# A mixture of experts with the layer norms at its two ends and its routing in one pass over the chunks, and roots as a power on GpSimd

## What is computed

```python
def _layernorm(x, axis=-1, eps=1e-05):
    m = jnp.mean(x, axis=axis, keepdims=True)
    v = jnp.var(x, axis=axis, keepdims=True)
    return (x - m) / jnp.sqrt(v + eps)

# stage 6, E = 8 experts, the two best kept
probs = jax.nn.softmax(jnp.einsum('bsh,eh->bse', x, router_w), axis=-1)
weights, indices = jax.lax.top_k(probs, K)
weights = weights / (weights.sum(axis=-1, keepdims=True) + 1e-06)
gate, up = jnp.split(jnp.einsum('bsh,ehi->bsei', x, w13), 2, axis=-1)
y = jnp.einsum('bsei,eih->bseh', jax.nn.silu(gate) * up, w2)

# stage 7 begins with
x = resid * lax.rsqrt(jnp.mean(resid * resid, -1, keepdims=True) + EPS) * norm_w

# stage 8, experts kept while the sorted probabilities sum to under 0.8
h = jax.nn.relu(jnp.einsum('bth,ehf->betf', x, W1) + b1[None, :, None, :])
y = jnp.einsum('betf,efh->beth', h, W2) + b2[None, :, None, :]
return jnp.einsum('bte,beth->bth', gate, y)
```

## Time and profile before

| | us |
|---|---|
| median of three runs | 2854.76 |
| lowest, highest | 2851.32, 2855.35 |
| the profiled execution | 2854.67 |
| its span, first to last instruction | 2852.9 |

### The profile page before, as it was taken

The page is one execution under the profiler, slowest core; times in us unless marked ns, Lnnn a source line. Parts: engine busy times, 40 slices in busy tenths (PEclk is TensorE's granted clock), DMA queues, the critical chain, the costliest instruction groups (busy, mean ns, idle before and its releaser), DMA issues.

```text
span 2852.9 us, 34984 instructions
## 1 busy us (share of the span) xinstructions
PE 2456.5 (86%) x12090; PEld 1765.4 (62%) x12090; DVE 1959.6 (69%) x3597; ACT 1447.9 (51%) x3042; POOL 941.1 (33%) x715
## 2 busy tenths in 40 slices
PE   6677778698999999999869999578888875999998
PEld 2554656586888888888847777223333324677776
DVE  6737555776666666666566665499999997666765
ACT  4321222597444444444345556444545443778787
POOL 1000000010222222222025554188888891122222
PEclk8668898899999999999889999689999987999999
DMA  4000000000000000000100000123222330000001
GB/s 170 0 1 0 1 1 1 1 1 15 1 1 1 1 1 1 1 1 1 60 1 1 1 1 1 42 78 89 83 83 85 79 97 1 1 1 1 1 1 30
DMA packets 31168, 66.84 MB, mean 23 GB/s; under 512 B 3200, under 2 KB 7312, under 8 KB 30480
## 3 DMA queue, kind: packets, MB, share of 16 engines
q1 hardware_dynamic: 30960, 64.59, 7.2%
q0 software_dynamic: 32, 0.02, 0.0%
HBM read 61.98 MB, written 2.62 MB: 23 GB/s over the span
## 4 chain that ended last, share of the span: by engine, by line
PE 43%; issue 21%; DVE 17%; POOL 12%; ACT 6%; DMA 0%; POOLq 0%; PEldq 0%; DVEq 0%; PEld 0%; ACTq 0%; SPq 0%
PE ps L192 40%; POOL XT L212 5%; POOL TMP L212 4%; DVE TMP L208 3%; PE ps L199 3%; POOL TMPr L212 3%; ACT TMP L203 2%; DVE TMP L2376 2%; DVE TMP L211 2%; DVE XK L208 1%; DVE TMPr L208 1%; ACT TMP L204 1%; DVE Wr L208 1%; DVE XT L207 1%; DVE SM L1138 1%
## 5 line engine op out<-in xcount | busy, mean ns | idle before, releaser
L192 PE MATMUL ps<-TMPr 128*128 128x512 f32 (+6 forms) x3936 | 1029.4, 409 | 53.7 <-DVE TMPr L208 34.0
L192 PEld LDWEIGHTS ps<-TMPr 128*128 128x128 f32 (+4 forms) x3936 | 727.7, 191 | 356.3 <-issue 175.4
L212 POOL TENSOR_TENSOR TMP<-TMP 128x512 f32<-128x512 f32 (+2 forms) x480 | 620.6, 1320 | 742.3 <-ACT TMP L203 464.8
L192 PE MATMUL ps<-TMP 128*128 128x65 f32 (+4 forms) x4320 | 529.5, 290 | 1.2 <-DVE TMP L207 0.5
L192 PEld LDWEIGHTS ps<-TMP 128*128 128x128 f32 (+3 forms) x4320 | 482.2, 193 | 62.1 <-issue 20.3
L192 PE MATMUL ps<-TMP,W 128*128 128x512 f32 (+5 forms) x720 | 393.6, 674 | 137.1 <-POOL TMP L212 38.6
L203 ACT ACTIVATE TMP<-ps,W 128x256 f32<-128x256 f32 (+2 forms) x512 | 274.3, 580 | 360.5 <-DVE TMP L208 192.7
L192 PEld LDWEIGHTS ps<-TMP,W 128*128 128x128 f32 (+3 forms) x720 | 132.0, 204 | 333.9 <-issue 170.0
L208 DVE TENSOR_TENSOR TMP<-ps,TMP 128x512 f32<-128x512 f32 (+1 forms) x434 | 251.0, 601 | 120.0 <-ACT TMP L203 68.4
L203 ACT ACTIVATE TMPr<-ps,W 128x512 fp32r<-128x512 f32 x352 | 242.6, 689 | 110.3 <-PE ps L192 88.9
L212 POOL TENSOR_TENSOR XT<-XT,XK 128x512 f32<-128x512 f32 x128 | 175.4, 1370 | 348.0 <-DVE XK L211 345.3
(11 more groups left out here) (172 smaller groups left out, 2766.1 us busy)
## 6 DMA issues: line engine op xcount, KB each, us to landing
TMP<-rows SPq DMA_DIRECT2D x168, 256.0 KB, 3.6
W<-wp SPq DMA_DIRECT2D x1, 4124.0 KB, 13.3
W<-wp SPq DMA_DIRECT2D x1, 3072.0 KB, 25.2
W<-wp SPq DMA_DIRECT2D x1, 2136.5 KB, 18.3
XT<-xT SPq DMA_DIRECT2D x4, 512.0 KB, 5.6
out<-XK SPq DMA_DIRECT2D x8, 256.0 KB, 2.3
W<-wp SPq DMA_DIRECT2D x1, 1993.0 KB, 13.8
TMP<-vecs SPq DMA_DIRECT2D x2, 512.0 KB, 3.9
```

The source lines that it names most:

```text
L192: return nc.tensor.matmul(out, lhsT, rhs, start=start, stop=stop, **k)
L212: gtt = lambda o, a, b, op: nc.gpsimd.tensor_tensor(o, a, b, op)
```

## The change

The norms 5 to 8, the routing, both mixtures of experts and the RMS norm are rewritten. `moe_pass(k)` takes the place of four parts and their fences for stage 6 (norm 5, routing, experts, norm 6, and the RMS norm) and of the like for stage 8. The norm ahead, the routing in four blocks of 1024 tokens and the rows of gates are steps of the plan inside expert 0; the norm behind and, in stage 6, the RMS norm are steps inside expert 7 and behind it.

- `centre` and `back` have one bank each. While experts 0 and 7 run, `up` has two pairs of banks in stage 6 and three banks in stage 8 (`few`); in between three pairs and five banks (`many`).
- The root and its reciprocal become one power of -0.5 on GpSimd, behind one or two small additions and a wait on GpSimd's own semaphore. The RMS norm's factor is taken from the layer norm's variance, so its own squares are gone. ACT no longer uses Sqrt in these stages; in stage 6 its exponentials now stand between Silu activations.
- Two `row` steps stand together, at every other chunk, with a gate behind them.
- The low parts of the weights move from DVE to POOL, the high part of expert 0 from DVE to ACT.
- In stage 8 seven additions of running sums become one scan. The exponential of A_log moves to the head of `scan_stage`. Wtap lies in the weights' memory, and its load waits until the last weights of stage 6 are split.

```diff
-    eps = SM[:, 479:480]
+    eps, power = SM[:, 479:480], SM[:, 436:444]
+    for k in range(1, 5):
-    ln_all = [x for k in range(1, LAST + 1) for x in ln_plans[k]]
+        p.append(("back", (k, 7)))
+    ln_all = [x for k in range(1, 1 + min(LAST, 4)) for x in ln_plans[k]]
...
-    MOE = {6: dict(nu=4, nd=2, ahead=3, g=4), 8: dict(nu=4, nd=4, ahead=4, g=6)}
+    MOE = {6: dict(nu=4, nd=2, ahead=3, g=4, route="rwT", rg=3), 8: dict(nu=4, nd=4, ahead=4, g=6, route="Wr", rg=6)}
+    ROUTE = {6: ("logits max shifted", "sum reciprocal probs top", "pair pair_reciprocal first", "replaced taken kept scaled"),
+             8: ("logits max shifted", "sum reciprocal probs top",
+                 "cum below always kept_probs fill kept_or_fill", "replaced taken kept")}
+    Wtap = w("w13")[:, 0:1024]
     def moe_plan(k):
-        nd, ahead = MOE[k]["nd"], MOE[k]["ahead"]
-        plan, second, pend, seen = [("row", (k, 0))], [], [], set()
+        nd, ahead, q = MOE[k]["nd"], MOE[k]["ahead"], k - 1
+        steps = lambda i, *names: [(n, (q, i)) for n in names]
+        route = lambda b, r: [("route", (k, b, r))]
+        def beside(i):
+            if i == 0:
+                return [steps(1, "square", "root", "norm"), steps(1, "back", "rows", "split") + steps(2, "centre"),
+                        steps(2, "square", "root", "norm"),
+                        steps(2, "back", "rows", "split") + steps(3, "centre")]
+            j, out = i + 2, [[], [], [], []]
+            if j < NCH:
+                out = [steps(j, "square", "root"), steps(j, "norm", "back"), steps(j, "rows", "split"),
+                       steps(j + 1, "centre") if j + 1 < NCH else []]
+            b = 0 if i == 1 else i // 2 if i % 2 == 0 else None
+            return [x + (route(b, r) if b is not None else []) for r, x in enumerate(out)]
+        plan = [("weights", (k, 0))] + steps(0, "centre", "square", "root", "norm") + steps(1, "centre") + steps(0, "back", "rows", "split")
         def down(a):
             _, e, i, c = a
-            if c == 0:
+            if e and c == 0:
                 plan.append(("gate", (k, e, i)))
-                if e == 0 and i + 1 < NCH:
-                    plan.append(("row", (k, i + 1)))
+            if e == 0 and c == nd - 1:
+                if i % 2 == 0:
+                    plan.extend([("row", (k, i)), ("row", (k, i + 1))])
+                plan.append(("gate", (k, e, i)))
             plan.append(("down", a))
+            if e == 7 and c == nd - 1:
+                behind.append([])
+                behind.append([("centre", (k, i))])
+                behind.append([("square", (k, i)), ("root", (k, i))])
+                behind.append([("norm", (k, i))] + ([("back", (k, i))] if k == 6 else [("store", (k, i))]))
+                if k == 6:
+                    behind.append([("rows", (k, i)), ("back2", (k, i)), ("rows2", (k, i))])
         for e in range(8):
             for i in range(NCH):
+                extra = beside(i) if e == 0 else None
                 for c in range(nd):
                     a = (k, e, i, c)
                     plan.append(("up", a))
+                    if e == 0:
+                        for part in extra[c * 4 // nd:(c + 1) * 4 // nd]:
+                            plan.extend(part)
+                    for _ in range(5 // nd):
+                        if behind:
+                            plan.extend(behind.pop(0))
                     if len(pend) > ahead - 1:
                         down(pend.pop(0))
-                if i == 1 and e + 1 < 8:
+                    if e == 0 and c == nd - 1 and (i == 0 or i % 2 and i < 6):
+                        plan.append(("logits", (k, (i + 1) // 2)))
+                if i == (4 if e == 0 else 1) and e + 1 < 8:
                     plan.append(("weights", (k, e + 1)))
+                if k == 6 and e == 7 and i == 4:
+                    plan.append(("taps", k))
         pend.append(second.pop(0))
         plan.append(("parts", pend[-1]))
         for a in pend:
             down(a)
+            for _ in range(5 // nd):
+                if behind:
+                    plan.extend(behind.pop(0))
+        for x in behind:
+            plan.extend(x)
         return plan
...
+        few, many = (2, 3) if k == 6 else (3, 5)
+        ubank, ubefore, holder = {}, {}, {}
+        for a in order:
+            n = few if a[1] in (0, 7) else many
+            ubank[a] = nth[a] % n
+            ubefore[a] = holder.get(nth[a] % n)
+            holder[nth[a] % n] = a
...
+        def up_free(e, a):
+            o = ubefore[a]
+            if o is not None:
+                e.wait_ge(*(mo_prod.at(o) if k == 6 else low(o)))
+            elif ubank[a] >= few:
+                e.wait_ge(*mn_x.at((q, NCH - 1)))
+                e.wait_ge(*mn_xl.at((q, NCH - 1)))
...
-                if step == "row":
+                if step == "centre":
+                    n, i = a
+                    if n == q and i:
+                        e.wait_ge(*mn_x.at((q, i - 1)))
+                    if n == k:
+                        e.wait_ge(*mg_add.at((k, 7, i)))
+                        if i:
+                            e.wait_ge(*(mn_x2 if k == 6 else mn_x).at((k, i - 1)))
+                        for o in borrowed if i == 0 else []:
+                            e.wait_ge(*(mo_prod.at(o) if k == 6 else low(o)))
+                    for j in range(4):
+                        r = mm(tile(pc, j), tile(src(a), 4 * i + j), w("cen"))
+                    r.then_inc(*mn_cen(a))
+                elif step == "back":
+                    n, i = a
+                    e.wait_ge(*mn_x.at(a))
+                    if i:
+                        e.wait_ge(*(mn_xl.at((n, i - 1)) if n == q else mn_xa2.at((n, i - 1))))
+                    for j in range(4):
+                        r = turn(tile(pt, j), tile(lf(i), j), w("ident"))
+                    r.then_inc(*mn_tr(a))
+                elif step == "back2":
+                    n, i = a
+                    e.wait_ge(*mn_x2.at(a))
+                    e.wait_ge(*mn_xa.at(a))
+                    for j in range(4):
+                        r = turn(tile(pt, j), tile(xf(i), j), w("ident"))
+                    r.then_inc(*mn_tr2(a))
...
-                if step == "row":
+                if step == "weights" and a[1] == 0:
+                    e.wait_ge(s_w[g], 16)
+                    for h, x in weights_high(a):
+                        last = acopy(h, x)
+                    last.then_inc(*me_hact(k))
+                elif step == "square":
+                    n, i = a
+                    junk = xf(i)
+                    e.wait_ge(*mn_cen.at(a))
+                    for j in range(4):
+                        c = 4 * i + j
+                        r = act(tile(junk, j), tile(pc, j), ACT.Square, scale=128 ** -0.5, acc=ss[:, c:c + 1])
+                    r.then_inc(*mn_sq(a))
+                elif step == "rows":
+                    n, i = a
+                    e.wait_ge(*mn_tr.at(a))
+                    acopy(ch(XT, i), pt).then_inc(*mn_xa(a))
+                elif step == "rows2":
+                    n, i = a
+                    e.wait_ge(*mn_tr2.at(a))
+                    act(ch(XK, i), pt, ACT.Copy, scale=w("normw")).then_inc(*mn_xa2(a))
+                elif step == "route" and a[2] == 0:
+                    e.wait_ge(*mr_dve.at((k, a[1], "shifted")))
+                    act(lg, lg, ACT.Exp).then_inc(*mr_act((k, a[1])))
...
-                if step == "row":
+                if step == "norm":
+                    n, i = a
+                    e.wait_ge(*mn_rs.at(a))
+                    tt(g3(lf(i), 4), g3(pc, 4), spread(rr(i)[:, 0:4], 128), ALU.mult).then_inc(*mn_x(a))
+                    if n == 6:
+                        tt(g3(xf(i), 4), g3(pc, 4), spread(rr(i)[:, 4:8], 128), ALU.mult).then_inc(*mn_x2(a))
+                elif step == "split":
+                    n, i = a
+                    e.wait_ge(*mn_xa.at(a))
+                    copy(ch(xh_all, i), ch(XT, i)).then_inc(*mn_xh(a))
+                    e.wait_ge(*mn_xh.at(a))
+                    minus(ch(xl_all, i), pt, ch(xh_all, i)).then_inc(*mn_xl(a))
...
+                elif step == "weights" and a[1]:
+                    if a[1] >= 2:
+                        e.wait_ge(*mo_down.at((k, a[1] - 2, NCH - 1, nd - 1)))
+                    for h, x in weights_high(a):
+                        last = copy(h, x)
...
         def pool(e):
+            nc.gpsimd.memset(WT.bitcast(F32), 0.0).then_inc(*mr_zero(k))
+            e.wait_ge(s_eps, 2)
             for step, a in plan:
-                if step == "parts" and k == 6 and odd(a):
+                if step == "weights":
+                    x = a[1]
+                    kh, kl = wb[x % 2]
+                    e.wait_ge(*(me_hdve.at(a) if x else me_hact.at(k)))
+                    if x >= 2:
+                        e.wait_ge(*mo_down.at((k, x - 2, NCH - 1, nd - 1)))
```

(22 more changed lines are left out.)

420 lines of the change are left out of this document (192 added, 228 removed).

## The result

The changed kernel takes **2995.39 us**, the median of four runs (2994.68 to 2995.48), against 2855.06 us of the kernel before on the same chip (2851.32 to 2857.06): a ratio of 1.0493, 95% interval 1.0474 to 1.0511. It is slower by 140 us. The prediction had slower, but by 40 us, and its range ended at 2940: the sign was right, the size wrong by a factor of three and a half.

A forecast was written before the change was run, and what follows sets the result against it. PE was taken as the bound inside the experts, with 89 us of PE idle to win around them. Fronts +17.0 and +16.7, ends +12.9 and -0.3, middle -6 made +40.3 on 2854.67: 2895.0 us, range 2835 to 2940.

The forecast's parts named there:

- rows in pairs: Expert 0: two `row` steps and a gate wait in line on one bank, 13.1 us in stage 6, 15.0 in stage 8.
- closed circles: Behind stage 6's last expert matmul: each next centre waits for `back2`, 6.15 us per chunk, 18.5 for three.
- PE work stays: Front of stage 6, norm 5 and expert 0: PE's own work unchanged at 60.6 us.
- rival C: Power slow as the filling, 2975 us, or PE at 1.2 GHz behind 25 stops, 15 us more; above 2940 together 0.08.
- The power: Root on POOL: 0.4 us for 4 or 8 columns, bounds 0.17 and 1.3.
- Chunks 1 and 2: Front of stage 6, normed beside the first chunk's two units: PE waits about 2.0 and 3.1 us.
- Chunks 3 to 7: Front of stage 6: PE stops 3.4 us before `back`, five times, 17.0 in all.
- End of stage 6: Norm 6 and RMS norm, from PE's last matmul before: 36.8 us become 49.7, so +12.9.
- End of stage 8: Expert 7 and what follows: -0.3 us, with seven centres (7.4) and 3 us of bank delays.
- Middle of stage 8: Weights' subtractions leave DVE, removing seven PE stops of about 0.9 us at splits: -6 us.
- rival D: Roots don't free ACT: Sqrt table loads go, eight for exponentials come; already in the sum, no separate chance.
- Rival A: Pieces interleave in both stretches, PE never stops long, only heads and ends idle: 56 us less, 2799 us; chance 0.20.

The follow-up runs named there:

- e11: The changed kernel with ten extra matmuls ahead of each `back` in the experts 0 and five ahead of second rows and their gates: 2964 us.
- e2: The changed kernel with a product in place of the power on the same columns, so no norm is computed: 2968 us, ratio 1.041 to the kernel before.
- e12: The changed kernel with every power made twice, the first result unused: 3031 us, ratio 1.0635 to the kernel before.
- e3: The changed kernel with `back` beside expert 0 two units (stage 6) or four (stage 8) behind its `centre`: 2955 us, ratio 1.0362 to the kernel before.
- e5: The changed kernel with norms out of the experts, over more banks, and each row one unit ahead of its gate: 2850 us, ratio 0.9995 to before.

## Why the prediction was wrong

Right were the sign, the mechanism (no lead between squares and `back`, rows in pairs, closed circles) and the middle. Wrong was the price. Over the stretches 108 us are missing, 148.7 against 40.3, in this order:

- **PE's busy time, 68 of the 108 us, and of these some 65 the clock.** This is the step that failed: the prediction held PE's work constant in the fronts ("PE work stays: 20.6 + 40.0 = 60.6 us", "PE work 20.1 + 53.7 = 73.8"). It gave the clock 3.8 us in the end of stage 6 and, as rival C, "0.6 us each, 15 us more" with a chance inside 0.08. Measured: +27.6, +27.8, +5.5 and +8.8 us of busy time on the same matmuls, 69.6 in all and 68.5 with the middle. By the trace's record of the clock half of PE's busy time at the low level is 16 us in the fronts and ends before and 81 after, 65 more. The 3.8 us do not lessen the miss: with them the forecast of PE's work for norm 6 and the RMS norm, 11.9 + 7.1 + 3.8, is just the 22.8 us of before. The row to see it by was there: the norm stage of before with half its time empty stood at 0.50, and a transposition took 1.11 us in it and not 0.66. I applied it to two chunks, and not to an expert 0 that I had just filled with 43 us of stops. The slip in rival C was to let each stop slow 0.6 us of work, when the clock stayed low for 88.7 of the first front's 147.5 us. The Trainium skill (Perfetto Trace Analysis, Matmul Optimizations) has "it's important that matmuls execute back-to-back in batches"; e11 agrees, with 20 us won per front by filling. The Trainium skill (TensorE: Matmul & The Clock Gate, HAM oscillation) tells of a kernel whose bursts of matmuls were shorter than the waits for DMA between them, so that each burst began at the low clock. This case is near that one and not the same: PE waits here for other engines, and its waits of 3.3 to 3.9 us before `back` are shorter than the 8.7 to 9.2 us of work ahead of the next one in chunks 3 and 4, at a granted clock of 0.70 over the front.
- **The power.** Priced at 0.4 us between 0.17 and 1.3; it lasts 1.04 for 4 columns, inside the bounds, and 1.67 for 8, outside. The bound was a subtraction on 512 columns, another operation: a product on these columns takes 0.20 and does not grow from 4 to 8 columns, while the power grows by 0.16 us for each. I had called it near the lower row "because the operand is small". 0.64 us for 14 roots and 1.27 for the 8 double ones make 19 us, which lie inside the stops below. e2 and e12 bear the size out: 0.84 and 1.46 us at these places are 23 us, and 27 were measured; 1.04 and 1.67 are 28, and 36 were measured, the rest by the clock or noise.
- **Fronts, the stops.** Chunks 1 and 2: 2.0 and 3.1 forecast, 2.59 and 3.38 measured. Chunks 3 to 7: 3.4 each, 3.30, 3.90, 3.88, 3.88 and 7.19 measured, with the power's excess inside, and in the last the weights' low parts on POOL, which the sum put at nothing. In stage 8 the seven were 2.68, 3.45, 3.13, 2.77, 4.93, 2.77 and 7.84 where 2.6 and 2.8 were forecast. Rows in stage 6: 13.1 forecast, 13.4 measured, in stage 8 18.1 for 15.0. Idle grew by 24.6 and 25.5 us where 17.0 and 16.7 were forecast: the mechanism stands, the size is half as much again. Over all stretches idle time grew by 80.2 us, twice the 40.3 of the forecast.
- **End of stage 6.** Stops in expert 7 were 22.6 us for 14.9. The circles of the last chunks took 8.5 and 8.95 us for 8.05 with the low clock; 26.4 us lie behind the last expert matmul (forecast 22.9). Each holds a power of 8 columns, 1.27 us over its price.
- **End of stage 8, the step that was wrong as a mechanism.** The prediction had "seven centres (7.4) and 3 us of delays on the three banks", and no wait of a `centre` for its own input. Each `centre` stands one unit behind its chunk's last `down` but needs DVE's product and POOL's 1.44 us addition. PE stopped 1.8 us at five of the eight and 15.1 us at all of them, and its busy time grew by 8.8, of which 5.7 are the clock by its record:

```profile
2967.66 1.44 POOL L212 TENSOR_TENSOR XT<-XT,XK 128x512 f32<-128x512 f32 x1 [1.87 <-DVE XK L211]
...
2969.16 1.16 PE L192 MATMUL ps<-W,XT 128*128 128x128 f32 x8 [1.81 <-POOL XT L212]
```

- **Middle of stage 8:** -6 forecast, -5.1 measured, no stop at the splits. The table loads (rival D) cost about what the sum had: the one in the third row pair lies in 5.13 us of stops, for 5.2 forecast.
- **Rival A** (all interleaves, 2799 us) had 0.20. Its "point", a lead of 3 us, was given in e3: `back` no longer waited in stage 6 and for 5.6 us in stage 8, and the kernel stood at 2955. Giving one step its lead moved the wait to the next one.

What would have shown me wrong did not occur: PE was about two thirds busy in the fronts, and 26.4 us lay behind the last matmul of stage 6. Two of the signs that the prediction gave for itself failed all the same: the `back` steps of chunks 3 to 7 of stage 6 came 13 to 21 us apart, where chunks of 10 to 13 us were forecast, and the power of 8 columns lay above 1.3 us. What stays open is why e2's front in stage 8 settled at a lower clock, and how much of the clock's 65 us is paid by each single stop; no run separates them. e5 changes the place of the norms and the number of banks together, so the share of the banks is open too.

## What to carry to other kernels

When a change puts waits into a stretch that PE had filled, price the work between the waits too, not the stops alone; ask of each stretch whether PE will still run on between them. Here a little under half of a front's work ran at the low clock, 61.8 us of busy time where 30.9 would do at full speed; all of it at the low clock would have been too much. Interleave work in whose chain PE takes part only with as many banks and as long a lead as it had alone; in e3 the lead by itself was not enough, and no run shows what the banks alone would give. Stages at whose edges PE stood idle anyway are better pipelined within themselves. Price an operation that no row shows by the kind of operation, not by its size. When work moves to an engine that lies in such a chain, ask what it will stand in front of: here the weights' low parts stood in front of a root.

## What the runs showed of the hardware

- More work on PE made the kernel faster: 110 matmuls of 128x512 more in each front, 20 us less in each.
- A power on GpSimd takes 1.04 us for 4 columns of 128 partitions and 1.67 for 8, a product of the same 0.20 and 0.20.
- Stretches of unchanged code differ between executions of otherwise like kernels by up to 19 us ahead of stage 6 and 9 us in the scan, so that effects of 10 us are seen in the stretch and not in one total.
